# A new opening for a cross-attention and mixture-of-experts kernel: zero rows by copy, first contexts masked on VectorE, statistics of x spread differently

## The reference

```
x = x + attention(layernorm(x), ctx)        # scores = q k / sqrt(8), masked where q or k token is off; softmax; @ Wc
x = x + moe(layernorm(x))                   # top 2 of 8 experts by router logits, softmax of the two logits
# expert: gelu(x @ w1[e].T + b1[e]) @ w2[e].T + b2[e]
```

## Time and profile before

| | us |
|---|---|
| median of 3 runs (lowest, highest) | 385.14 (384.53, 386.89) |
| span of the profiled execution | 383.3 |
| PE busy | 309.2 (81%) |
| DVE busy | 255.3 (67%) |
| POOL busy | 241.7 (63%) |
| ACT busy | 232.6 (61%) |

### The profile page before, as it was taken

How to read it: one execution, slowest core, us unless ns; L and a number is a source line. 1 busy time by engine, 2 the same in 40 slices (tenths; PEclk the granted TensorE clock), 3 DMA queues, 4 the chain that set the end, 5 groups by cost and what they waited for, 6 DMA issues and landing times.

```text
span 383.3 us, 11559 instructions
## 1 busy us (share of the span) xinstructions
PE 309.2 (81%) x3720; PEld 251.8 (66%) x3720; DVE 255.3 (67%) x750; ACT 232.6 (61%) x566; POOL 241.7 (63%) x387
## 2 busy tenths in 40 slices
PE   1633878998997979797988089999999999999930
PEld 0211546666666657475765079889999999998930
DVE  7406678889788889788868826785545554556752
ACT  1311366879787878877788037556666666666520
POOL 7796335352487786858486786577877666665550
PEclk9999989999999999999999559999999999999995
DMA  5589454566474463442110386575986766669846
GB/s 152 93 212 232 130 138 114 145 111 175 124 201 129 146 170 101 130 130 58 36 54 31 96 262 185 167 223 163 275 239 196 232 202 208 204 172 353 271 119 192
DMA packets 61850, 62.95 MB, mean 164 GB/s; under 512 B 14109, under 2 KB 46260, under 8 KB 61632
## 3 DMA queue, kind: packets, MB, share of 16 engines
q1 hardware_dynamic: 55168, 50.34, 48.6%
q0 software_dynamic: 4320, 8.47, 6.4%
q10 hardware_dynamic: 2304, 3.41, 2.8%
HBM read 37.65 MB, written 11.88 MB: 129 GB/s over the span
## 4 chain that ended last, share of the span: by engine, by line
PE 45%; POOL 21%; issue 14%; DVE 7%; DMA 5%; SPq 4%; ACT 2%; DVEq 0%; POOLq 0%; ACTq 0%
PE sexp L1244 16%; PE smax L1235 15%; POOL dispatch_d L706 10%; PE smax L1040 3%; SPq L443 3%; DVE shift L1315 2%; PE tail L1084 2%; POOL rstd L666 2%; POOL qpart L619 2%; DMA stacks<-result_d 1%; DMA kmask<-mask_dram 1%; POOL shift L626 1%; PE feed L1031 1%; PE feed L1016 1%; POOL xq L614 1%
## 5 line engine op out<-in xcount | busy, mean ns | idle before, releaser
L1315 DVE TENSOR_REDUCE shift<-smax 128x4 f32<-128x512 f32 x128 | 87.0, 684 | 35.8 <-PE smax L1040 34.8
L792 POOL DMA_INDIRECT result_d<-y_out,stacks x71 | 70.7, 995 | 31.3 <-issue 29.5
L706 POOL DMA_INDIRECT dispatch_d<-rows_out,row_i x64 | 63.5, 993 | 34.2 <-DVE rows_out L1444 16.8
L871 ACT ACTIVATE probs<-sexp 128x512 f32<-128x512 f32 x128 | 74.2, 592 | 10.1 <-PE sexp L1048 9.1
L1235 PE MATMUL smax<-probs,w_ring 128*128 128x128 f32 x568 | 77.8, 281 | 1.6 <-ACT probs L978 1.0
L1244 PE MATMUL sexp<-w_sb,probs 128*128 x568 | 77.0, 279 | 2.6 <-ACT probs L982 2.4
L1768 DVE TENSOR_TENSOR probs<-smax,b_cols 128x512 f32<-128x512 f32 x71 | 49.1, 691 | 42.4 <-PE smax L1235 38.5
L1244 PEld LDWEIGHTS sexp<-w_sb,probs 128*128 128x128 f32 x568 | 69.8, 194 | 5.0 <-issue 4.9
L1235 PEld LDWEIGHTS smax<-probs,w_ring 128*128 128x128 f32 x568 | 70.7, 196 | 3.3 <-issue 2.9
L982 ACT ACTIVATE probs<-probs 128x512 f32<-128x512 f32 x71 | 44.8, 631 | 37.6 <-DVE probs L1768 37.5
L1040 PE MATMUL smax<-stacks 64*128 64x128 bf16 x512 | 47.9, 225 | 12.9 <-DMA stacks<-kpart 7.0
(11 more groups left out here) (215 smaller groups left out, 511.4 us busy)
## 6 DMA issues: line engine op xcount, KB each, us to landing
w_ring<-w_t_dram SPq DMA_DIRECT2D x71, 256.0 KB, 3.6
stacks<-kpart SPq DMA_DIRECT2D x48, 128.0 KB
stacks<-qpart SPq DMA_DIRECT2D x48, 128.0 KB
stacks<-dispatch_d SPq DMA_DIRECT2D x71, 65.0 KB, 3.5
stacks<-result_d ACTq DMA_DIRECT2D x12, 256.0 KB, 4.4
ctx<-ctx_t_dram SPq DMA_DIRECT2D x8, 256.0 KB, 3.7
w_sb<-w_t_dram SPq DMA_DIRECT2D x8, 256.0 KB, 3.4
out_dram<-xw SPq DMA_DIRECT2D x8, 256.0 KB, 3.3
```

The lines of the kernel that those rows point to most:

```text
L706: nc.gpsimd.indirect_dma_start(out=dispatch_d, out_offset=bass.IndirectOffsetOnAxis(ap=row_i[r % RR][:, k, b:b + 1], axis=0), in_=rows_out ...
L792: nc.gpsimd.indirect_dma_start(out=result_d, out_offset=bass.IndirectOffsetOnAxis(ap=xg[r][:, D + 1:D + 2].bitcast(U32), axis=0), in_=y_ou ...
L871: nc.scalar.activation(dst, sexp[hp][:], ACT.Exp).then_inc(exp_done, 1)
L1315: nc.vector.tensor_reduce(shift4[n % 2][:, hp, 0, 4 * m:4 * m + 4], smax[hp][:], AX.X, ALU.max, negate=True).then_inc(max_taken, 1)
```

## The change

- `stacks` isn't cleared any more. A tile `no_rows` of 16 partitions by 2 KB is set to zero on DVE, and copied by DMA into slot 7 alone: on ACT's queue for group 0 (each of the 16 rows 8 times, 256 KB), on SP's queue between the k parts and the q parts of group 1 for groups 1 and 2 together (16 times, 512 KB). PE waits for these at s = 0 and s = 4.
- The masking of contexts 0 and 1 moves from POOL to DVE, straight from the 8-bit mask, without the cast before it. The power of part 0 is now POOL's first real work. The clearing of `query_terms` moves from DVE to POOL.
- Loads: context 0, the mask's columns and then the weights on ACT's queue; the second mask row load, x and context 1 earlier on SP's; the third part of x (now 4 batches) in the first burst, ahead of the mask terms; the other two parts at s = 1 and s = 2 of the loop. `mask_d` is stored behind the q parts of group 0, and its reader, the load of context 2 with its mask, moves ahead of group 1's k parts.
- `LN_PARTS` has five parts: batches 0 to 3, 4 to 7, 8 to 11, 12 to 15, 16 to 31. The third is done ahead of the loop, the fourth at the end of slot 4, the last in pieces of 6, 5 and 5 batches at the ends of slots 5 to 7.
- `values[1]` is preset on POOL at s = 4, the constants at s = 6 (before: s = 3) and DVE's part of them at s = 7 (before: 5); a w2 load comes at the end of a group of slots.

```diff
-        LN_PARTS = ((0, GB), (GB, 2 * GB), (2 * GB, 4 * GB), (4 * GB, BATCH))
+        LN_PARTS = ((0, GB), (GB, 2 * GB), (2 * GB, 3 * GB), (3 * GB, 4 * GB), (4 * GB, BATCH))
...
-            sp.wait_ge(cleared, 1)
...
+            zero_to = stacks[SLOTS - 1::SLOTS, 2 * SW:].rearrange("p (o c) -> p o c", c=GT)
+            sp.dma_start(zero_to, no_rows[:].rearrange("p (o c) -> p o c", o=1).to_broadcast([2 * SLOTS, zero_to.shape[1], GT])).then_inc(
+                zero_rows[1], 16)
...
+                if s in (1, 2):
+                    load_x(s + 2)
...
-            clear_stack(0)
-            mask_ctx(0)
             query_scale(0)
             scale_rows(0)
+            query_scale(1)
             split_low(0, krest, kpart, k_split)
-            query_scale(1)
-            mask_ctx(1)
             scale_rows(1)
             split_low(0, qrest, qpart, q_split)
-            clear_stack(1)
+            prepare_values(0)
             split_low(1, krest, kpart, k_split)
...
+            query_scale(2)
             split_low(1, qrest, qpart, q_split)
...
+            act.wait_ge(no_rows_set, 1)
+            zero_to = stacks[SLOTS - 1::SLOTS, 0:2 * SW].rearrange("p (o c) -> p o c", c=GT)
+            act.dma_start(zero_to, no_rows[:].rearrange("p (o c) -> p o c", o=1).to_broadcast([2 * SLOTS, zero_to.shape[1], GT])).then_inc(
+                zero_rows[0], 16)
...
+                nc.vector.tensor_tensor(ctx_m[g][:], ctx_sb[g][:], kmask8[g][:], ALU.mult).then_inc(ctx_masked, 1)
...
-                if s == 0:
-                    dve.wait_ge(x_loaded[2], 16)
-                    row_stats(2 * GB, 4 * GB)
-                    row_moments(2)
...
+                if s == 4:
+                    dve.wait_ge(x_loaded[3], 16)
+                    row_stats(3 * GB, 4 * GB)
+                    row_moments(3)
+                if s in (5, 6, 7):
+                    if s == 5:
+                        dve.wait_ge(x_loaded[4], 16)
+                    row_stats((16, 22, 27)[s - 5], (22, 27, 32)[s - 5])
+                    if s == 7:
+                        row_moments(4)
```

More of the change, by code:

```diff
@@ L245, in xattn_ffn @@
         masks_loaded = sem("masks_loaded")
-        x_loaded = [sem(f"x_loaded{i}") for i in range(4)]
+        mask_cols_loaded = sem("mask_cols_loaded")
+        x_loaded = [sem(f"x_loaded{i}") for i in range(5)]
         kv_loaded = sem("kv_loaded")
@@ L258, in xattn_ffn @@
         mask_stored = sem("mask_stored")
-        kmask_cast = sem("kmask_cast")
+        no_rows_set = sem("no_rows_set")
+        zero_rows = [sem(f"zero_rows{i}") for i in range(2)]
         terms_stored = sem("terms_stored")
@@ L414, in _, with load_x, load_kmask @@
         def _(sp):
-            sp.dma_start(xs[:, 0:GB, :], x[:, 0:GB, :]).then_inc(x_loaded[0], 16)
-            sp.dma_start(mask_rows8[:], mask).then_inc(masks_loaded, 16)
-            sp.dma_start(mask_cols8[:], mask_t).then_inc(masks_loaded, 16)
+            def load_x(part):
+                at = slice(*LN_PARTS[part])
+                sp.dma_start(xs[:, at, :], x[:, at, :]).then_inc(x_loaded[part], 16)
+            def load_kmask(g):
+                to, of = (kmask8[g], mask) if g < 2 else (kmask[g % RING], mask_d)
+                sp.dma_start(to[:], of[g:g + 1, :].to_broadcast([P, GT])).then_inc(ctx_loaded[g % RING], 16)
             def load_ctx(g):
                 sp.dma_start(ctx_sb[g % RING][:], ctx_t[:, g * GT:(g + 1) * GT]).then_inc(ctx_loaded[g % RING], 16)
-                to, of = (kmask8[g], mask) if g < 2 else (kmask[g % RING], mask_d)
-                sp.dma_start(to[:], of[g:g + 1, :].to_broadcast([P, GT])).then_inc(ctx_loaded[g % RING], 16)
+                load_kmask(g)
             def load_terms(g):
@@ L449, in load_shift @@
                 sp.dma_start(rows[:, :, n % GB * SEQ:(n % GB + 1) * SEQ], shift_t[n % 2][:]).then_inc(shift_loaded[n % 2], 16)
-            load_ctx(0)
-            sp.dma_start(xs[:, GB:2 * GB, :], x[:, GB:2 * GB, :]).then_inc(x_loaded[1], 16)
+            load_x(0)
+            load_kmask(0)
+            sp.dma_start(mask_rows8[:], mask).then_inc(masks_loaded, 16)
+            load_x(1)
             load_ctx(1)
+            load_x(2)
             sp.wait_ge(mask_prep, MASK_STEPS)
@@ L457, in _ @@
                 sp.dma_start(query_terms_d[:, h], query_terms).then_inc(terms_stored, 16)
-            sp.dma_start(mask_d, mask_rows[:]).then_inc(mask_stored, 16)
-            sp.wait_ge(cleared, 1)
-            load_part(0, 0, "k")
-            load_part(0, 1, "k")
-            load_part(0, 2, "k")
+            for part in range(3):
+                load_part(0, part, "k")
             sp.wait_ge(terms_stored, 64)
             load_terms(0)
-            sp.dma_start(xs[:, 2 * GB:4 * GB, :], x[:, 2 * GB:4 * GB, :]).then_inc(x_loaded[2], 16)
             for part in range(3):
                 load_part(0, part, "q")
-            sp.wait_ge(cleared, 2)
+            sp.dma_start(mask_d, mask_rows[:]).then_inc(mask_stored, 16)
             load_terms(1)
-            for part in range(3):
-                load_part(1, part, "k")
             sp.wait_ge(mask_stored, 16)
@@ L474, in _ @@
             for part in range(3):
+                load_part(1, part, "k")
+            zero_to = stacks[SLOTS - 1::SLOTS, 2 * SW:].rearrange("p (o c) -> p o c", c=GT)
+            sp.dma_start(zero_to, no_rows[:].rearrange("p (o c) -> p o c", o=1).to_broadcast([2 * SLOTS, zero_to.shape[1], GT])).then_inc(
+                zero_rows[1], 16)
+            for part in range(3):
                 load_part(1, part, "q")
-            sp.dma_start(xs[:, 4 * GB:, :], x[:, 4 * GB:, :]).then_inc(x_loaded[3], 16)
-            sp.wait_ge(cleared, RING)
             for s in range(BATCH + 1):
@@ L500, in _ @@
                     load_ctx(g)
-                if s % GB == 0 and s // GB < EXPERTS:
+                if s % GB == GB - 1:
                     sp.dma_start(w2_sb[:, s // GB:s // GB + 1], w2_t[:, s // GB:s // GB + 1]).then_inc(w2_loaded, 16)
@@ L1474, in _ @@
             row_moments(1)
+            split_rest(0, feed, krest, kpart, k_split)
+            mask_first_ctx(1)
+            dve.wait_ge(x_loaded[2], 16)
+            row_stats(2 * GB, 3 * GB)
+            row_moments(2)
             split_rest(0, prep, qrest, qpart, q_split)
```

71 lines of the change are left out of this document (33 added, 38 removed).

## The result

| | median, us (lowest, highest) | profiled span, us |
|---|---|---|
| before | 385.08 (382.49, 387.4), 20 runs | 383.3 |
| changed | 382.72 (379.96, 386.08), 20 runs | 380.8 |

The ratio is 0.9935, with a 95% interval of 0.9912 to 0.9959. The change makes the kernel 2.5 us faster by the ratio and by the spans (2.4 by the medians); 5.1 were forecast. The measured time lies inside the range. Single executions of either kernel can be over 1.5% slower than the fastest, at other granted clocks; all ratios of this document leave those out.

What follows compares the result with a forecast made beforehand. SP's full queue bounds the opening, POOL second. Gains of 5.3 at slot 5 and 1.8 from DVE, less 2.0 for late statistics, give -5.1; 383.3 - 5.1 + 1.84 = 380.0 us, range 376.0 to 384.5.

Steps and rivals of the forecast that it cites:

- Step 1: Opening: with work taken from DVE, the last mask term is done and its stores begin 0.7 us earlier.
- two-input rule: Opening: DVE operations with two SBUF inputs and GpSimd reads hold a lock; without it the mask-term gain would be 1.2 us.
- Step 2: SP's queue: two DMAs taken from ahead of the q parts give 1.8 us, an empty queue 2.6; first scores at 24.9.
- Step 3: First scores to first turned maxima: POOL splits without waiting for preset and power, 4.4 us; first turn 9.5 earlier, at 29.3.
- Step 4: Queue ahead of slot 3: 512 KB of zero rows from 16 partitions take 5.0 us; slot 3 begins 5.6 earlier.
- the 52 GB/s of rows 5: DMA rate of mask terms from 8 partitions in the profile before, scaled to 104 GB/s for 16 partitions.
- Rival A: Zero rows move at the queue's usual rate, 2.3 us; slot 5 begins 8.0 earlier, 376.7 us in all; chance 0.25.
- Step 5: Loads of x in the loop: slot 5 begins 5.3 us earlier, DVE's work there gives 1.8 more; shift 7.1.
- the queue's 3.1 MB: Loads behind the zero rows, ahead of the third maxima that slot 5 needs: 13.8 us at 228 GB/s.
- Step 6: Slots 5 to 7: late statistics add 4.2 us of DVE work, of which 2.0 are lost (0 to 4.2).
- a clock under 1.00: Sign that the forecast is wrong: a granted clock under 1.00 in slots where it was 1.00; no size given.
- C: Slots 4 to 7 pay DVE's 4.2 us in full, or the opening gains 2 less: 382.6 us; chance 0.14.

Runs made afterwards that it cites:

- Experiment 3: Changed kernel with the masked columns made on DVE behind the moments of the first x instead of ahead of its statistics; ratio to the kernel before 0.9900.
- Experiment 6: Kernel before with only the store of mask_d moved behind group 0's q parts and the load of x behind context 1; ratio 0.9944.
- Experiment 1: Changed kernel with the zero rows read from all 128 partitions instead of 16, one 256 KB copy per group; 378.31 us, ratio to the kernel before 0.9818.
- experiment 4: Changed kernel with the 512 KB copy of zero rows made twice, the second behind the first's landing; one execution, 387.04 us.
- experiment 5: Kernel before with only the last 16 batches' statistics moved to the ends of slots 5 to 7 and the constants on DVE to slot 7; ratio 1.0004.
- experiments 9 to 11: Wide zero rows, late columns and even statistics with constants early (0.9808) and without that (0.9899); then the changed kernel with even statistics (no ratio).
- experiment 11: Changed kernel with its last 16 statistics in four pieces of 4 at the ends of slots 5 to 8; 419.22 us in 4 runs, no ratio.
- experiment 2: Changed kernel with statistics and moments spread over slots 3 to 7 and the constants at slots 3 and 4; 385.21 us, ratio to the kernel before 0.9986.
- experiments 3, 5 and 7: The last of these: changed kernel with zero rows from 128 partitions and masked columns behind the first moments; ratio to the kernel before 0.9860.

## Why the prediction was half right

**Step 1 (0.7 us from the mask terms' start): didn't come.** `ctx_m` on DVE took the 0.68 that I took, but I had not priced the load of the mask's columns as second on ACT's queue: the columns are DVE's first instruction, and the wait of 2.63 us holds all behind it. Experiment 3 gives back 0.6. (The two-input rule that the prediction takes from the skill isn't what rows 3 and 4 show: `mask_cols` has one input. The last section has the form that fits.)

**Step 2 (first scores 5.1 earlier with step 1): 4.7.** Right in the sum, by luck in its terms. SP came to the q parts 1.1 earlier (19.59 for 20.64) and not 2.5, since step 1 gave nothing and the six k parts now took 5.32 us in place of 4.38. The last q part, issued at 22.80, had landed 2.5 us later; 3.5 were forecast, and it was 6.1 before. Experiment 6 has 3.8 for step 2 alone in the kernel before.

**Step 3 (turn 1 9.5 earlier): 8.9.** Right. Experiment 6 shows why it needed both: step 2 alone brings 2.5 of it.

**Step 4 (zero rows 5.0 us, slot 3 5.6 earlier): slot 3's first scores at 42.09, 4.7 earlier.** The mechanism and the price are those of the prediction: the copy from 16 partitions moves 100 GB/s (104 forecast), about half the queue's rate. The way to the price was lucky: the 52 GB/s of rows 5 are a mean with a pause in it, and while the mask terms' stores moved, at 11 to 13 us, it was 66, which by the same rule gives 132 GB/s and 4.0 us. The miss is in the landing of the maxima: SP issued them at 38.82 (39.3 forecast), and they landed 3.2 us later, not 1.9. At turn 3 only 4.1 were left, since slot 3's first scores ran at the low clock (0.3 us a matmul) and before at the high one (0.2). Experiment 1 takes the cause away and gives 2.2 us at turn 3 and 2.5 at turn 6 (5.0 less 2.3 is 2.7), experiment 4 doubles it. Rival A has no standing as the change was made, and names what the wide copy brings. The Trainium skill (SBUF — State Buffer, "Door 1: The DMA port swizzle") agrees with the 100 GB/s: its bound of about 109 and the estimate of 4.8 us were nearer than the queue's usual rate. That the 52 GB/s agree with two ports, as the prediction has it, rests on the same pause: half of the 109 is about 55, and the stores moved 66.

**Step 5 (slot 5 7.1 earlier): 5.96 at turn 6.** 4.66 were there at turn 5 (5.3 forecast for slot 5's start, 4.8 measured: 51.92 for 56.68), and 1.30 came by the statistics that left slot 4 (1.8 forecast, 1.31 in experiment 5). But the queue's 3.1 MB, from which the 5.3 was worked out, didn't set slot 5: from 46 to 56 us PE waited for ACT and DVE and for no DMA. Slot 5 carries on the gain of slot 3's start, and that both sums came out alike was luck. Where the forecast let DVE work in a wait for the queue, there was none.

**Step 6 (2.0 us for the late statistics): 3.4** (turns 6 to 10). This is the step that failed, by its size. The forecast took 2.4 us of DVE's idle time off 4.2 us of work, as if amounts could be set against each other. The runs show two other things in its place. Four to six statistics and the moments at a slot's end stand ahead of the next row's maxima and of `qrest`, behind which ACT holds an exponential: 1.9 us over four slots (21.30 less 19.42). It falls to 1.5 with even pieces and the moments and power a slot later, to 0.9 when the statistics are laid between the maxima besides, and doesn't change when 0.9 us of constants go away; the last 0.9 is unexplained. And while PE waits, the clock can fall, which goes with another 1.3 to 1.5 us (1.5 in the changed kernel). I had named a clock under 1.00 as something that would make the prediction wrong, and given it no term.

The errors add up: 0.6 at turn 5, 0.5 at turn 6, 1.4 between turns 6 and 10, together the 2.5 between forecast and result. The range held because it reached to C (382.6), which had the right time by luck: in C all of DVE's 4.2 us count, where 1.9 did and the clock made up the rest. A range worked out around the forecast alone, 378 to 382, would have missed.

## What to carry to other kernels

Ask of a tile that a DMA copies how many partitions it is read from: 512 KB from 16 partitions cost 2.2 to 2.5 us more than from 128, since the first maxima stood behind it on the queue. When work moves onto a nearly full engine, don't subtract idle time from it; write down what stands behind it in that engine's order and in the order of the engine that it feeds, since 0.9 us in one place cost nothing, and 0.86 at the end of each of three slots cost 0.5 more than the same work between the maxima. Where such a wait leaves PE idle in the middle of a loop, add a fall of its clock as a term with its own chance: here 1.3 to 1.5 us in each of four traces.

Beside a kernel before of 385.1 us the wide copy alone took 378.31 us, the changed kernel 382.72. The other versions with wide zero rows have ratios of 0.978 to 0.990, taken in other sets of runs. Which of them is the best these runs can't tell: their intervals overlap.

## What the runs showed of the hardware

One and the same chip ran at two speeds at two times: experiments 1 to 4 beside a kernel before of 385.1 us, experiments 9 to 11 beside one of 421.7. The first ten slots show no such slowing: turns 6 to 10 take 19.42 us before and in experiment 6, and 22.6 to 22.8 with a fall of the clock in experiments of either time. The granted clock was lower behind 105 us (0.93 for 150 to 200 us in experiment 11, 1.00 in the changed kernel), and at 300 to 350 us, with 1.00 in both, PE made 393 matmuls in experiment 11 and 442 in the changed kernel. So times are compared within one set of runs alone, and places in a trace by their distance to each other.

A small load (4 KB) behind a 256 KB one on ACT's queue landed at 6.4 us in the changed kernel, where the first x on SP's queue was there at 5.0 (experiment 3).

SP is held by a queue that drains slowly, not only by its waits: six issues took 3.8 us on a free queue and 7.95 behind the narrow copy.

DVE's `moment_sum` (L1308), 0.17 us in the changed kernel, took 1.25 in experiment 2 beside POOL's preset of `values` and ended with it. In the kernel before, the 1.12 of `mask_cols` (rows 3) in place of 0.18 in the changed kernel are of the same sort, beside `ctx_m` on POOL. The Trainium skill (SBUF — State Buffer, "Who interferes with whom") says that such an operation (`tensor_scalar`) can run in a mode that shares a port pair with GpSimd, and that the one that comes second then stands still until the first has ended; the rows agree, though none of them shows the mode itself.

The same idle stretch of PE (1.62 of 4 us busy) was followed by a fall of the clock in experiments 3, 5 and 7 and not in experiment 1, nor in experiment 4 (1.63). Each kernel was profiled once, so how often it falls is open. What it costs was much the same each time: turns 6 to 10 took 22.57 to 22.82 us in place of 21.30, and 32 matmuls that fell into it 1.93 to 1.94 us in place of 1.08 (the changed kernel, experiments 3 and 5).
